# Retention block and mixture of experts on one core: slot biases summed on eight partitions, joined slot products, VectorE's order and two loads moved

## The chip, the cores and the metric

The kernel is written by hand for one core of a Trainium2 chip. Time is the device time of one execution in microseconds (us), and lower is better. Five engines work beside each other and meet only at semaphores: PE (TensorE, matrix products, whose weight loads have a row of their own, PEld), DVE (VectorE), ACT (ScalarE), POOL (GpSimd) and SP, which here issues the DMAs. Data lies in SBUF (128 partitions), products land in eight PSUM banks of 128 x 512 float32.

## The reference, cut to what matters

```python
x = L0_attn_x                                   # (4, 1024, 256)
x = x + attn(layernorm(x), ...)                 # retention with 16 heads of 16
x = x + ffn(layernorm(x), ...)

# attn: q, k, v = x @ W.T; scores decayed by head; y = (q k^T * decay / 4) v
mean, var = y.mean(axis=(1, 3)), y.var(axis=(1, 3))     # over time, per head
yn = (y - mean) / sqrt(var + EPS) * gn_weight + gn_bias
return yn @ W_o.T

# ffn: one shared expert, and 8 experts of which each token takes 2
shared = silu(xf @ sw1 + sb1) * (xf @ sw3 + sb3) @ sw2 + sb2
for k in range(2):
    exp_ids = (tok * 11 + k * 7919) % 8         # fixed by the token's number
    h = gelu(einsum('enc,ech->enh', xs, w1) + b1)
    y = einsum('enh,ehc->enc', h, w2) + b2
    out = out.at[sort_idx].add(y)
return (shared + out / 2) / 2
```

## The kernel before, in words

A token's two experts follow from its number modulo 8, so the host sorts each batch's 1024 tokens into eight *slots* of 128; slot s meets experts s and s-1. Every product is made in float32r with operands split in a high and a low part (`hi` and `lo`), as hi·hi + lo·hi + hi·lo: three matrix products where one stands in the reference (`split_product`, L305 in the profile's rows).

**First phase** (up to 213 us of the span): four batches in four parts of 256 tokens, so 16 parts, `step(0)` to `step(15)` on each engine. In step h, PE makes k and q of part h+1 (L305), state sums (L389), the two terms of y (L404, L413), transposes (L354 for k, L315 for x), v of part h+1, and the scores of part h+1 (L375). In the last two parts of a batch PE also multiplies the batch before by W_o (`output`). DVE in a step masks scores, adds and carries the state (`add_state`; `carry_state`, L827), scales k and q, makes the statistics of x of part h+3 (`ln_sums`), applies the layer norm (`ln_apply`, L781), and makes y's low part (`low_y`, L836), y's statistics (`y_sums`, L841) and x's low part for part h+2 (`low_x`, L786). `ln_apply` needs the reciprocal root that POOL makes from `ln_sums`; `low_y` needs ACT's high part of y; PE's next k needs `low_x`. From step 13 on, `ln2_sums` and `ln2_apply` (L948) do the same for the second layer norm, whose input `xl` is read back from a DRAM scratch.

POOL also makes low parts of the FFN's weights (L1087), adds the output bias to the residual, and in steps 0 and 1 forms the bias of each slot, `(sb2 + (b2[s] + b2[s-1]) / 2) / 2`, on all 128 partitions: b2 is loaded with each partition holding all eight rows, and `slot_bias_sums` (L1134) and `slot_bias_means` (L1138, L1140) work on 128 x 2048 numbers.

SP issues the loads in a written order: `load_x(h)` waits for the transposes of part h-4, and each is followed by a piece of the FFN's weights; `next_xres` loads 1 MB of residual, `store_x1` stores 1 MB.

**Second phase**: the shared expert and the experts. Per batch PE runs eight products `shared`, eight `expert`, and eight `slot`, the last of 8 chunks of contraction by 3 products of 256 columns, 24 in all, into the first half of `o_bank`; `add_slot` on DVE (L986) adds the bank to `xr`, which then is stored. Batches are three turns of a hardware loop and a last turn written out. Slot s waits until slot s-2's bank was read (`o_ready`).

Of the kernel before, what the change touches and what calls it, by code (L numbers as in the profile page):

```python
# [55 lines left out]

def moe_retention(nc, xa, xs, wattn, gnw, gnb, sw1, sw3, sw2, w1, w2, sb1, sb3, b1, sb2, b2, decay, masks, out):
    x1_dram = nc.dram_tensor("x1_scratch", [NBATCH, P, NE * D], F32).ap()
    last = NBATCH - 1

    with ExitStack() as ctx:
# [20 lines left out]
        sw2_split = SplitWeight(nc, ctx, "sw2", [P, MS, D], lo_first=True)  # L82
# [23 lines left out]
        w2_split = SplitWeight(nc, ctx, "w2", [P, NE, MR, D], lo_first=True)  # L106

        with ExitStack() as phase1:
# [17 lines left out]
            for i in range(2):  # L126
                yhi[i] = sb_1(f"yhi{i}", [P, GROUPS, NE, P], F32R)
                if i:

                    with nc.sbuf_tensor("slot_scratch", [P, 2, D], F32) as slot_scratch:  # L130
                        pass
                ylo[i] = sb_1(f"ylo{i}", [P, GROUPS, NE, P], F32R)
# [5 lines left out]
            sbias, bias7 = slot_scratch[:, 0, :], slot_scratch[:, 1, :]  # L138
# [21 lines left out]
        def expert_buffer(e):  # L160
# [28 lines left out]
        bias_ready, bias_part = sem("bias_ready"), sem("bias_part")  # L189
# [4 lines left out]
            sem(n) for n in ("h1_done", "h3_done", "sil_ready", "gf_ready", "ghi_ready", "glo_ready"))  # L194
        e_done, gelu_ready, ehi_ready, elo_ready, slot_done, biased, o_ready = (
# [15 lines left out]
        def _(sp):  # L211
# [53 lines left out]
            next_xres(0)  # L265
# [8 lines left out]
            load_ffn(10)  # L274
            sp.wait_ge(t_done, PARTS - 2)
# [23 lines left out]
        def _(pe):  # L299
            def split_product(o, w, x, first=True, last=True):  # L300

                n = len(w)
                for c in range(n):
                    for j, (l, r) in enumerate(((0, 0), (1, 0), (0, 1))):
                        mm = nc.tensor.matmul(o, w[c][l], x[c][r], start=first and c == 0 and j == 0,  # L305
                                              stop=last and c == n - 1 and j == 2)
                return mm
# [214 lines left out]
            def slot(b, s):  # L522
# [6 lines left out]
                w = [(sw2_split.hi[:, m, :], sw2_split.lo[:, m, :]) for m in range(MS)]  # L529
# [228 lines left out]
        def _(dve):  # L758
# [71 lines left out]
            def low_y(h):  # L830
                b, s = h // NSUP, h % NSUP
                at = slice(s * (SUPER // NE), (s + 1) * (SUPER // NE))
                if h == NSUP:
                    dve.wait_ge(bias_ready, 1)
# [4 lines left out]
            def y_sums(h):  # L839
                for g in range(GROUPS):  # L840
# [46 lines left out]
            def step(h):  # L887
# [25 lines left out]
                if b and s == 0:  # L913
                    gn_eps(b - 1, p_bank[0])
                if h + 3 < PARTS:
                    ln_apply(h + 3)
                elif h + 3 == PARTS:
                    ln2_apply(0, 0)
# [3 lines left out]
                low_y(h)  # L922
                y_sums(h)
                if h + 2 < PARTS:
                    low_x(h + 2)
                elif h + 2 == PARTS:
                    ln2_apply(0, 1)
# [54 lines left out]
            def add_slot(b, s):  # L982
# [3 lines left out]
                nc.vector.tensor_tensor(xr[:, s, :], o_bank[s % 2][:, 0:D], xr[:, s, :], ALU.add).then_inc(o_ready, 1)  # L986
# [70 lines left out]
        def _(pool):  # L1057
# [31 lines left out]
            def step(h):  # L1089
# [16 lines left out]
                if h == 0:  # L1106
                    slot_bias_sums()
                if h == 1:
                    slot_bias_means()
# [16 lines left out]
            def slot_bias_sums():  # L1126

                pool.wait_ge(bias_landed, 32)
                nc.gpsimd.tensor_scalar(sbias, sbias, 0.5, None, ALU.mult)
                nc.gpsimd.tensor_copy(bias7, slot_bias[:, NE - 1, :]).then_inc(bias_part, 1)  # L1130
                for i, s in enumerate(reversed(range(NE))):
                    pool.wait_ge(bias_part, i + 1)
                    before = slot_bias[:, s - 1, :] if s else bias7
                    nc.gpsimd.tensor_tensor(slot_bias[:, s, :], slot_bias[:, s, :], before, ALU.add).then_inc(bias_part, 1)  # L1134

            def slot_bias_means():
                pool.wait_ge(bias_part, NE + 1)
                nc.gpsimd.tensor_scalar(slot_bias[:], slot_bias[:], 0.25, None, ALU.mult).then_inc(bias_part, 1)  # L1138
                pool.wait_ge(bias_part, NE + 2)
                nc.gpsimd.tensor_tensor(slot_bias[:], slot_bias[:], sbias.unsqueeze(1).broadcast_to([P, NE, D]), ALU.add).then_inc(bias_ready, 1)  # L1140
# [11 lines left out]
            pool.wait_ge(bias_ready, 1)  # L1152
# [69 lines left out]
```

## Time and profile before

| | |
|---|---|
| median of 3 runs | 455.54 us (454.89 to 456.48) |
| the profiled execution's own time | 458.03 us |
| its span | 456.2 us |
| PE busy | 442.1 us, 97% of the span |
| DVE, ACT, POOL busy | 286.2, 216.7, 109.3 us |
| granted TensorE clock, mean | 0.989 |

The span is the stretch from the first to the last instruction in the trace; the execution's own time holds 1.8 us around it. The profiled execution took 2.5 us more than the median of the three runs without a profile. Times in rows are us from the span's start.

### The profile page before, as it was taken

How to read it: one execution, taken by the hardware profiler on the slowest of the kernel's cores; microseconds unless marked ns; L12 is line 12 of the kernel's file. 1: busy time of each engine (PE TensorE's matmuls, PEld its weight loads, DVE VectorE, ACT ScalarE, POOL GpSimd, SP SyncE). 2: the span in 40 equal slices, each digit the busy share in tenths (PEclk: the TensorE clock that was granted, in tenths of full speed). 3: DMA queues.
4: the chain of work that ended last, by engine and by line, in shares of the span. 5: the costliest groups of instructions: out<-in, count | busy, mean ns of one | idle time of the engine just before them, and what ended most of it. 6: DMA issues, size and time to landing. Idle time of an engine off the chain costs nothing.

```text
span 456.2 us, 14962 instructions
## 1 busy us (share of the span) xinstructions
PE 442.1 (97%) x6574; PEld 408.3 (90%) x6574; DVE 286.2 (63%) x653; ACT 216.7 (47%) x416; POOL 109.3 (24%) x81
## 2 busy tenths in 40 slices
PE   6999798999999999999999999999999999999997
PEld 4999798999899998898889999899998899988997
DVE  6888786767777777867565633856347473465321
ACT  3556356544664657544428233463334643336521
POOL 1168322522134223414180200402004010040000
PEclk9999898999999999899999999999999999999999
DMA  8512242201632042100622011400115001120011
GB/s 261 210 51 74 70 158 79 71 24 53 208 121 72 5 134 103 49 3 37 242 102 83 1 47 56 177 0 0 46 46 184 0 0 46 43 95 0 1 47 46
DMA packets 9990, 34.75 MB, mean 76 GB/s; under 512 B 1744, under 2 KB 2128, under 8 KB 8272
## 3 DMA queue, kind: packets, MB, share of 16 engines
q1 hardware_dynamic: 9504, 33.15, 20.6%
q8 instruction: 45, 0.74, 0.7%
q10 hardware_dynamic: 432, 0.79, 0.6%
q14 instruction: 9, 0.07, 0.0%
HBM read 25.54 MB, written 8.39 MB: 74 GB/s over the span
## 4 chain that ended last, share of the span: by engine, by line
PE 90%; DVE 4%; issue 3%; POOL 1%; DMA 1%; ACT 1%; POOLq 0%; DVEq 0%; ACTq 0%
PE bank L305 70%; PE bank L375 5%; PE bank L404 3%; PE bank L413 3%; PE bank L389 3%; PE bank L354 2%; PE bank L492 2%; PE bank L315 1%; DMA xin<-xa 1%; DVE state L827 1%; PE bank L429 1%; DVE xlo L786 1%; POOL w_lo L1087 1%; DVE y_st L841 0%; DVE ylo L836 0%
## 5 line engine op out<-in xcount | busy, mean ns | idle before, releaser
L708 ACT ACTIVATE xres<-bank,r1b 128x256 f32<-128x256 f32 x64 | 26.7, 468 | 55.6 <-PE bank L305 55.6
L305 PE MATMUL bank<-x2hi,sw_lo 128*128 128x512 f32 x128 | 51.0, 398 | 0.0
L305 PE MATMUL bank<-x2hi,sw_hi 128*128 128x512 f32 x128 | 50.8, 397 | 0.0
L693 ACT ACTIVATE sil<-bank,s1b 128x512 f32<-128x512 f32 x32 | 22.0, 688 | 60.4 <-PE bank L305 60.4
L305 PE MATMUL bank<-x2lo,sw_hi 128*128 128x512 f32 x128 | 50.2, 392 | 0.0
L968 DVE SCALAR_TENSOR_TENSOR gf<-bank,s3b,sil 128x512 f32<-128x512 f32 x32 | 23.9, 746 | 34.6 <-PE bank L305 34.6
L305 PE MATMUL bank<-xhi,wqkv_hi 128*128 128x256 f32 x128 | 40.2, 314 | 3.9 <-DVE xlo L786 3.7
L802 DVE TENSOR_TENSOR pm<-bank,msk 128x512 f32<-128x512 f32 x64 | 39.8, 683 | 5.9 <-PE bank L375 5.8
L625 ACT ACTIVATE keo<-kT,msk 128x512 f32<-128x512 f32 x32 | 21.3, 714 | 46.0 <-DVE kT L791 46.0
L986 DVE TENSOR_TENSOR xr<-bank,xr 128x256 f32<-128x256 f32 x32 | 13.5, 423 | 41.9 <-PE bank L305 41.9
L1121 POOL TENSOR_TENSOR xr<-xr,slot_bias 128x2048 f32<-128x2048 f32 x4 | 18.5, 4625 | 82.2 <-DMA xr<-x_scratch 82.2
L974 DVE TENSOR_TENSOR glo<-gf,ghi 128x512 fp32r<-128x512 f32 x32 | 34.8, 1087 | 3.7 <-ACT ghi L697 3.7
L305 PE MATMUL bank<-xhi,wqkv_lo 128*128 128x256 f32 x128 | 37.0, 289 | 0.0
L305 PE MATMUL bank<-xlo,wqkv_hi 128*128 128x256 f32 x128 | 36.9, 289 | 0.0
L305 PE MATMUL bank<-x2lo,w_hi 128*128 128x256 f32 x128 | 36.2, 283 | 0.0
L305 PE MATMUL bank<-x2hi,w_hi 128*128 128x256 f32 x128 | 36.2, 283 | 0.0
L305 PE MATMUL bank<-x2hi,w_lo 128*128 128x256 f32 x128 | 36.2, 283 | 0.0
L980 DVE TENSOR_TENSOR elo<-xres,ehi 128x512 fp32r<-128x512 f32 x32 | 22.1, 691 | 22.5 <-ACT ehi L712 22.5
L305 PE MATMUL bank<-sw_hi,ghi 128*128 128x256 f32 x128 | 36.2, 282 | 0.0
L305 PE MATMUL bank<-w_hi,elo 128*128 128x256 f32 x128 | 36.1, 282 | 0.0
L305 PE MATMUL bank<-w_lo,ehi 128*128 128x256 f32 x128 | 36.0, 281 | 0.0
L305 PE MATMUL bank<-w_hi,ehi 128*128 128x256 f32 x128 | 35.9, 281 | 0.0
(120 smaller groups left out, 1265.9 us busy)
## 6 DMA issues: line engine op xcount, KB each, us to landing
xin<-xa SPq DMA_DIRECT2D x16, 256.0 KB, 3.2
w_raw<-w SPq DMA_DIRECT2D x8, 512.0 KB, 4.2
xres<-xs SPq DMA_DIRECT2D x4, 1024.0 KB, 5.0
x_scratch<-xres SPq DMA_DIRECT2D x4, 1024.0 KB, 5.5
xl<-x_scratch SPq DMA_DIRECT2D x8, 512.0 KB, 5.5
xr<-x_scratch SPq DMA_DIRECT2D x4, 1024.0 KB, 4.9
out<-xr SPq DMA_DIRECT2D x7, 512.0 KB, 2.6
sw_raw<-sw SPq DMA_DIRECT2D x3, 512.0 KB, 5.0
```

Source lines behind the costliest of these rows:

```text
L305: mm = nc.tensor.matmul(o, w[c][l], x[c][r], start=first and c == 0 and j == 0, stop=last and c == n - 1 and j == 2)
L375: mm = nc.tensor.matmul(p_bank[p][:, o:o + CH], keo[at, c, g, :, :], qT[h % 2][at, g, c * CH:(c + 1) * CH], start=True, stop=True)
L389: mm = nc.tensor.matmul(a_bank[32 * p:32 * p + 32, o:o + n * 32].rearrange("p (n e) -> p n e", n=n), kexp[:, c, r, :], vexp[h % 2][:, c, r ...
L404: nc.tensor.matmul(y_bank[at, o:o + CH], state[h % 2][at, g, c, :], qT[h % 2][at, g, c * CH:(c + 1) * CH], start=(c == first and g == 0), ...
L625: cp = nc.scalar.activation(keo[:, :, :, odd, :], kT[:].rearrange("p g (c j) -> p c g j", c=CPS), ACT.Copy, scale=parity[:, odd:odd + 1])
L693: nc.scalar.activation(sil[i % 2][:], h1_bank[i % 2][:], ACT.Silu, bias=s1b[:, m:m + 1]).then_inc(sil_ready, 1)
L708: ge = nc.scalar.activation(hf[q % 2][:, m, :], e_bank[q % 4][:, m * 2 * P:(m + 1) * 2 * P], ACT.Gelu, bias=r1b[:, e, m:m + 1])
L802: nc.vector.tensor_tensor(pm[p][:], p_bank[p][:].rearrange("p (a i) -> p a i", i=CH), causal.unsqueeze(1).broadcast_to([P, CPS * GROUPS, C ...
L968: nc.vector.scalar_tensor_tensor(gf[i % 3][:], h3_bank[i % 2][:], s3b[:, m:m + 1], sil[i % 2][:], ALU.add, ALU.mult).then_inc(gf_ready, 1)
L974: nc.vector.tensor_tensor(glo[half][:, m, :], gf[i % 3][:], ghi[half][:, m, :].bitcast(F32), ALU.subtract).then_inc(glo_ready, 1)
L980: nc.vector.tensor_tensor(elo[k][:], hf[q % 2][:], ehi[k][:].bitcast(F32), ALU.subtract).then_inc(elo_ready, 1)
L1121: nc.gpsimd.tensor_tensor(xr[:], xr[:], slot_bias[:], ALU.add).then_inc(biased, 1)
```

## The change

Five edits.

1. **Slot biases.** b2, b2 shifted by one row and sb2 are loaded onto eight partitions (one for each slot), POOL does four operations of 8 x 256 in step 1, the result is stored to a DRAM scratch, and later broadcast to 128 partitions by a DMA of 1 MB, behind the last piece of weights and ahead of the first `xl` load.
2. **The residual's first load** (`next_xres(0)`, 1 MB) moves forward, from behind `load_ffn(4)` to behind the small bias loads of part 2's group.
3. **DVE's order in a step**: `low_y` and `y_sums` go ahead of `ln_apply` (or `ln2_apply`) and of the residual. In step 15 `y_sums` and `gn_channels` go ahead of the residual, and `low_y` behind it.
4. **Joined slot products**: high and low part of w2 and sw2 lie in one tensor, and one product of 512 columns takes both against the high part of the activations. A slot has 16 products.
5. **`add_slot`** adds the two halves of the bank, one after the other, with a semaphore between them.

```diff
+class JoinedWeight:
+    def __init__(self, nc, ctx, name, shape):
+        p, n, *rest = shape
+        with ExitStack() as at:
+            at.enter_context(nc.sbuf_tensor(name + "_before", shape, F32))
+            self.raw = at.enter_context(nc.sbuf_tensor(name + "_raw", shape, F32))
+        self.both = ctx.enter_context(nc.sbuf_tensor(name + "_both", [p, 2 * n, *rest], F32R))
+        self.hi, self.lo = self.both[:, 0:n], self.both[:, n:2 * n]
...
-            sp.dma_start(slot_bias[:], b2.partition_broadcast(P)).then_inc(bias_landed, 16)
-            sp.dma_start(sbias, sb2.partition_broadcast(P)).then_inc(bias_landed, 16)
+            sp.dma_start(bias_in[:, 0, :], b2).then_inc(bias_landed, 16)
+            sp.dma_start(bias_in[1:NE, 1, :], b2[0:NE - 1]).then_inc(bias_landed, 16)
+            sp.dma_start(bias_in[0:1, 1, :], b2[NE - 1:NE]).then_inc(bias_landed, 16)
+            sp.dma_start(bias_in[:, 2, :], sb2.partition_broadcast(NE)).then_inc(bias_landed, 16)
             load_x(6)
             sp.dma_start(wo_raw[:], wattn[:, 3]).then_inc(w_landed[3], 16)
             for dst, src in ((s1b, sb1), (s3b, sb3), (r1b, b1)):
                 sp.dma_start(dst[:], src).then_inc(c2_landed, 16)
+            next_xres(0)
             load_x(7)
...
             load_ffn(3)
+            sp.wait_ge(bias_part, 4)
+            sp.dma_start(bias_dram, bias_in[:, 0, :]).then_inc(bias_stored, 16)
             load_x(9)
             load_ffn(4)
-            next_xres(0)
...
             load_ffn(10)
+            sp.wait_ge(bias_stored, 16)
+            sp.dma_start(slot_bias[:], bias_dram.partition_broadcast(P)).then_inc(slots_landed, 16)
             sp.wait_ge(t_done, PARTS - 2)
             load_xl(0, 0)
...
+            def wide_product(o, x, w):
+                n = len(w)
+                for c in range(n):
+                    hi, lo = x[c]
+                    nc.tensor.matmul(o.rearrange("p (k d) -> p k d", k=2), hi, w[c], start=c == 0, stop=c == n - 1, skip_group_check=True)
+                    mm = nc.tensor.matmul(o[:, 0:D], lo, w[c][:, 0, :], start=False, stop=c == n - 1, skip_group_check=True)
+                return mm
...
-                    w += [(w2_split.hi[:, e, m, :], w2_split.lo[:, e, m, :]) for m in range(MR)]
-                split_product(o_bank[s % 2][:, 0:D], g, w).then_inc(slot_done, 1)
+                    w += [w2_split.both[:, e::NE, m, :] for m in range(MR)]
+                wide_product(o_bank[s % 2][:], g, w).then_inc(slot_done, 1)
...
                 dve.wait_ge(slot_done, b * NE + (s + 1))
-                nc.vector.tensor_tensor(xr[:, s, :], o_bank[s % 2][:, 0:D], xr[:, s, :], ALU.add).then_inc(o_ready, 1)
+                nc.vector.tensor_tensor(xr[:, s, :], o_bank[s % 2][:, 0:D], xr[:, s, :], ALU.add).then_inc(o_half, 1)
+                dve.wait_ge(o_half, b * NE + (s + 1))
+                nc.vector.tensor_tensor(xr[:, s, :], o_bank[s % 2][:, D:2 * D], xr[:, s, :], ALU.add).then_inc(o_ready, 1)
...
+            def slot_biases():
+                pool.wait_ge(bias_landed, 64)
+                at = bias_in[:, 0, :]
+                nc.gpsimd.tensor_tensor(at, at, bias_in[:, 1, :], ALU.add).then_inc(bias_part, 1)
...
+                nc.gpsimd.tensor_scalar(at, at, 0.5, None, ALU.mult).then_inc(bias_part, 1)
```

The order on DVE is taken from the compiled programs. In step 13, the second part of the last batch, DVE issued before (`xl` is the second layer norm's input, `ylo` y's low part, `y_st` its statistics, `xlo` the low part that PE's next k and v products need, `pm` the masked scores of the next step):

```order
L936 BN_STATS ln_st<-xl 128x6 x4
L940 BN_AGGR ln_mv<-ln_st 128x2 x4
L943 TENSOR_SCALAR ln_ve<-ln_mv 128x4
L948 TENSOR_SCALAR xl<-xl,ln_mv,ln_r 128x256 x4
L836 TENSOR_TENSOR ylo<-bank,yhi 128x16x32
L841 BN_STATS y_st<-bank 128x6 x2
L786 TENSOR_TENSOR xlo<-bank,xhi 128x512
```

and now:

```order
L972 BN_STATS ln_st<-xl 128x6 x4
L976 BN_AGGR ln_mv<-ln_st 128x2 x4
L979 TENSOR_SCALAR ln_ve<-ln_mv 128x4
L866 TENSOR_TENSOR ylo<-bank,yhi 128x16x32
L872 BN_STATS y_st<-bank 128x6 x2
L984 TENSOR_SCALAR xl<-xl,ln_mv,ln_r 128x256 x4
L816 TENSOR_TENSOR xlo<-bank,xhi 128x512
```

The application of the layer norm, which waits for POOL's `ln_r`, now stands behind the two operations on y; `xlo` stays last.

On SP, around the constants of part 2's group, the order was (`wo_raw` is W_o, `s1b`, `s3b` and `r1b` small biases):

```order
L256 DMA wo_raw<-wattn 128x512
L258 DMA s1b<-sb 128x4
L258 DMA s3b<-sb 128x4
L258 DMA r1b<-b 128x16
L215 DMA xin<-xa 128x512
```

and it is now:

```order
L273 DMA wo_raw<-wattn 128x512
L275 DMA s1b<-sb 128x4
L275 DMA s3b<-sb 128x4
L275 DMA r1b<-b 128x16
L243 DMA xres<-xs 128x2048
L229 DMA xin<-xa 128x512
```

The 1 MB load of the residual follows the constants with no wait between them. At the end of the loads of the first phase SP now has, where the third of these rows was not there before:

```order
L229 DMA xin<-xa 128x512
L234 DMA w_raw<-w 128x1024
L295 DMA slot_bias<-bias_scratch 128x2048
L253 DMA xl<-x_scratch 128x1024
L238 DMA x_scratch<-xres 128x2048
```

So 1 MB of broadcast now follows 0.75 MB of x and weights at once, and the load of `xl` keeps its own wait behind it.

## Rows read from the trace of the kernel before

**Rows 1.** The page's chain of work that ended last, by engine.
```profile
PE 90%; DVE 4%; issue 3%; POOL 1%; DMA 1%; ACT 1%; POOLq 0%; DVEq 0%; ACTq 0%
```

**Rows 2.** The chain in order of time, 38 to 56 us: start, us, what.
```profile
40.29 0.83 PE bank L389 x64
41.12 1.64 PE bank L305 x12
...
51.59 2.89 PE bank L305 x12
54.47 1.12 PE bank L389 x64
```

**Rows 3.** The timeline, 42 to 52 us: start, us, engine, line, operation; idle time before it.
```profile
42.06 4.59 POOL L1140 TENSOR_TENSOR slot_bias<-slot_bias,slot_scratch 128x2048 f32<-128x2048 f32 x1
43.39 3.44 DVE L827 TENSOR_SCALAR state<-state,msk 128x32 f32<-128x32 f32 x2
51.59 0.54 PE L305 MATMUL bank<-xhi,wqkv_hi 128*128 128x256 f32 x1 [2.38 <-DVE xlo L786]
```

**Rows 4.** Busy times by stretch: us, PE, PEld, DVE, ACT, POOL, PEclk, DMA share, GB/s.
```profile
51.60:55.50 3.90, 3.90 (x76) 3.66 (x76) 2.33 (x4) 0.00 (x0) 0.63 (x1) 0.56 0.02 6
```

**Rows 5.** POOL's timeline in step 0.
```profile
27.08 5.61 POOL L1134 TENSOR_TENSOR slot_bias<-slot_bias 128x256 f32<-128x256 f32 x7
```

**Rows 6.** The chain, 59 to 75 us.
```profile
59.86 1.44 PE bank L305 x12
...
69.79 1.43 issue
...
72.43 2.57 PE bank L305 x12
```

**Rows 7.** SP's timeline: the issues of three loads.
```profile
28.40 0.43 SPq L258 DMA_DIRECT2D r1b<-b  x1
...
62.61 0.43 SPq L229 DMA_DIRECT2D xres<-xs  x1
...
138.30 0.43 SPq L220 DMA_DIRECT2D w_raw<-w  x1
```

**Rows 8.** DMA queues, 61.9 to 68.6 us, then 68.6 to 69.7: packets, MB, share.
```profile
q1 hardware_dynamic: 423, 1.80, 76.2%
...
q8 instruction: 1, 0.02, 5.4%
```

**Rows 9.** DVE and PE in step 13, from the timeline.
```profile
187.78 1.38 DVE L948 TENSOR_SCALAR xl<-xl,ln_mv,ln_r 128x256 f32<-128x256 f32 x4 [1.12 <-POOL ln_r L1117]
...
191.08 0.38 PE L305 MATMUL bank<-xhi,wqkv_hi 128*128 128x256 f32 x1 [0.76 <-DVE xlo L786]
```

**Rows 10.** The chain, 188 to 195 us.
```profile
189.16 0.60 DVE ylo L836
189.76 0.67 DVE y_st L841 x2
...
191.08 2.52 PE bank L305 x12
193.59 1.44 PE bank L389 x64
```

**Rows 11.** PE behind step 15, from the timeline.
```profile
216.96 0.38 PE L419 MATMUL bank<-y_mv,msk 128*128 128x2 f32 x2 [0.55 <-DVE y_mv L847]
```

**Rows 12.** PE's timeline: first and last of 46 products of 256 columns, then of 22 of 512.
```profile
227.03 0.28 PE L305 MATMUL bank<-wo_lo,yhi 128*128 128x256 f32 x1
...
232.42 0.28 PE L305 MATMUL bank<-wo_lo,yhi 128*128 128x256 f32 x1
220.79 0.40 PE L305 MATMUL bank<-x2lo,sw_hi 128*128 128x512 f32 x1
...
225.70 0.39 PE L305 MATMUL bank<-x2lo,sw_hi 128*128 128x512 f32 x1
```

**Rows 13.** The end of the chain.
```profile
453.17 0.42 DVE xr L986
```

More of the change, by code:

```diff
@@ L81, in moe_retention @@
         sw3_split = SplitWeight(nc, ctx, "sw3", [P, CB, HS])
-        sw2_split = SplitWeight(nc, ctx, "sw2", [P, MS, D], lo_first=True)
+        sw2_split = JoinedWeight(nc, ctx, "sw2", [P, MS, D])
         msk = sb("msk", [P, MASK_W])
@@ L105, in moe_retention @@
         w1_split = SplitWeight(nc, ctx, "w1", [P, NE, CB, HR], lo_first=True)
-        w2_split = SplitWeight(nc, ctx, "w2", [P, NE, MR, D], lo_first=True)
+        w2_split = JoinedWeight(nc, ctx, "w2", [P, NE, MR, D])
         with ExitStack() as phase1:
@@ L128, in moe_retention @@
                 if i:
-                    with nc.sbuf_tensor("slot_scratch", [P, 2, D], F32) as slot_scratch:
+                    with nc.sbuf_tensor("slot_scratch", [P, 3, D], F32) as slot_scratch:
                         pass
@@ L137, in moe_retention @@
             o_bias = sb_1("o_bias", [P, D])
-            sbias, bias7 = slot_scratch[:, 0, :], slot_scratch[:, 1, :]
+            bias_in = slot_scratch[0:NE]
         xl = sb("xl", [P, NE, D])
@@ L188, in moe_retention @@
         xl_landed = [sem(f"xl{i}_landed") for i in range(2)]
-        bias_ready, bias_part = sem("bias_ready"), sem("bias_part")
+        bias_part, bias_stored, slots_landed = sem("bias_part"), sem("bias_stored"), sem("slots_landed")
         ln2_stats, ln2_aggr, ln2_var, ln2_rstd, xn2_ready = (
@@ L194, in moe_retention @@
             sem(n) for n in ("h1_done", "h3_done", "sil_ready", "gf_ready", "ghi_ready", "glo_ready"))
+        o_half = sem("o_half")
         e_done, gelu_ready, ehi_ready, elo_ready, slot_done, biased, o_ready = (
@@ L528, in slot @@
                 g = [(ghi[half][:, m, at], glo[half][:, m, at]) for m in range(MS)]
-                w = [(sw2_split.hi[:, m, :], sw2_split.lo[:, m, :]) for m in range(MS)]
+                w = [sw2_split.both[:, m::MS, :] for m in range(MS)]
                 if s == 0:
@@ L833, in low_y @@
                 if h == NSUP:
-                    dve.wait_ge(bias_ready, 1)
+                    dve.wait_ge(bias_stored, 16)
                 dve.wait_ge(yhi_ready, h + 1)
@@ L839, in y_sums @@
             def y_sums(h):
+                dve.wait_ge(yhi_ready, h + 1)
                 for g in range(GROUPS):
@@ L914, in step @@
                     gn_eps(b - 1, p_bank[0])
+                if h + 1 == PARTS:
+                    y_sums(h)
+                    gn_channels(b)
+                    for j in (2, 3):
+                        residual(b - 1, j, p_bank[j])
+                    low_y(h)
+                    return
+                low_y(h)
+                y_sums(h)
                 if h + 3 < PARTS:
                     ln_apply(h + 3)
-                elif h + 3 == PARTS:
-                    ln2_apply(0, 0)
+                else:
+                    ln2_apply(0, h + 3 - PARTS)
                 if b and s >= 2:
@@ L1105, in step @@
                     pool.wait_ge(xn2_ready, h + 4 - PARTS)
-                if h == 0:
-                    slot_bias_sums()
                 if h == 1:
-                    slot_bias_means()
+                    slot_biases()
                 if b and s == 1:
@@ L1124, in experts @@
                     ln2_power(b + 1, 1)
[L1126 to L1140, printed above, removed]
+            def slot_biases():
+                pool.wait_ge(bias_landed, 64)
+                at = bias_in[:, 0, :]
+                nc.gpsimd.tensor_tensor(at, at, bias_in[:, 1, :], ALU.add).then_inc(bias_part, 1)
+                pool.wait_ge(bias_part, 1)
+                nc.gpsimd.tensor_scalar(at, at, 0.5, None, ALU.mult).then_inc(bias_part, 1)
+                pool.wait_ge(bias_part, 2)
+                nc.gpsimd.tensor_tensor(at, at, bias_in[:, 2, :], ALU.add).then_inc(bias_part, 1)
+                pool.wait_ge(bias_part, 3)
+                nc.gpsimd.tensor_scalar(at, at, 0.5, None, ALU.mult).then_inc(bias_part, 1)
             nc.gpsimd.memset(minus_half[:], -0.5).then_inc(half_set, 1)
@@ L1151, in _ @@
             bias_xres(last)
-            pool.wait_ge(bias_ready, 1)
+            pool.wait_ge(slots_landed, 16)
             with pool.Fori(0, last) as b:
```

5 lines of the change are left out of this document (1 added, 4 removed).

## Prediction

> **What bounds the kernel now.** I read the page's chain first: PE holds 90% of it, DVE 4%, POOL and DMA 1% each, and 3% is "issue" [rows 1]. So PE's own work sets nearly all of the time. An edit pays only where it shortens that work or closes one of the few gaps in it. I then went through the chain in order of time and marked each piece that is not PE's, and each PE piece that takes longer than its twins. Four places remain.
>
> *The gap in step 2.* POOL's last operation on the slot biases takes 4.59 us from 42.06. DVE's `carry_state`, two instructions on 32 numbers each, starts at 43.39 and takes 3.44 us, ending when POOL ends [rows 3]. Everything behind it on DVE is late, `xlo` last, and PE waits 2.38 us at 51.59 [rows 3]. The engine then runs for 3.9 us at a granted clock of 0.56 [rows 4], which is mostly the lower level of 1.2 GHz. Twelve products take 2.89 us where 1.64 is usual, the state sums 1.12 where 0.83 is usual [rows 2]: 1.5 us more. The place costs 2.4 + 1.5 = 3.9 us.
>
> *The gap in step 4.* PE stops for 1.43 us with no engine to release it, in the middle of a run of like products with no wait between them. The twelve products after it take 2.57 us, against 1.44 for the same twelve a step earlier [rows 6], so the clock fell again; with the transposes behind them I count 1.5 us, as in step 2. I looked for what the queues did. 1.80 MB moved between 61.9 and 68.6 us, at 76% of all 16 engines, and no packet of the instruction queue; directly behind it, in 68.6 to 69.7, comes one of 16 KB [rows 8]. The last load of that burst is `next_xres(0)`, issued at 62.61 [rows 7]. My reading is that PE's next piece of code stood behind the burst. The place costs 2.9 us.
>
> *The gap in step 13.* DVE idles 1.12 us for POOL's `ln_r`, then applies the layer norm in 1.38 us [rows 9], then makes `ylo` (0.60) and `y_st` (0.67) [rows 10], then `xlo`; PE waits 0.76 us for that [rows 9]. The lower clock follows: 2.52 against 1.64 and 1.44 against 0.83 [rows 2, 10], 1.5 us. The place costs 2.3 us.
>
> *The gap behind step 15*: 0.55 us for the last statistics of y [rows 11].
>
> **The change part by part.**
>
> *Slot biases on eight partitions.* In step 0 the seven additions of 256 columns took 5.61 us, 0.8 each [rows 5]. Four operations of that width should take 3.2 us. Fewer partitions need not make them shorter (lower bound some 0.4 each, if they do). They begin where the first of the two wide operations began, so that the four are over before the second one's old start at 42.06. The `carry_state` that was held starts at 43.39 [rows 3], and is free. The gap in step 2 goes: **-3.9 us** (bounds -2.4, if another gap still draws the lower clock, and -3.9). What follows in its place is `xlo` as in other steps, with no wait in them. SP waits for POOL's fourth operation before `load_x(9)`. Queued behind are all later loads; but SP comes to that wait behind `load_x(8)`, which needs a transpose of PE's step 2, a whole step after POOL's four operations, so it costs 0. If POOL were late, x of part 9 would be late next, which is used four steps on.
>
> The Trainium skill says the same of the pair of engines (SBUF — State Buffer, section "SBUF: two separate sides"): GpSimd and a VectorE operation in a two-port mode hold a shared port for a whole instruction, and the other blocks. By that rule also the four small operations could hold DVE, but for one of them at a time; the 3.44 us agree.
>
> *The order on DVE.* In step 13 `ylo` and `y_st` (1.27 us together) now fill the 1.12 us of waiting for `ln_r`. `xlo` is therefore ready some 1.1 us sooner, which covers PE's 0.76. The gap and its slow stretch go: **-2.3 us**. Bounds: 0, if DVE comes late from something else, and -2.3. The margin is only 0.3. In step 15 the statistics pass the residual: **-0.6** (0 to -0.6). In the other steps PE has no wait on DVE that ended a gap, so the order changes nothing there; what hides it is PE's scores, which stand between the transposes and the products that need `xlo`. Against it: in step 14 the residual's two additions stand behind the 1.38 us application and y's operations, and the next scores need their banks: **+0.1** (0 to 0.5).
>
> *Joined products.* Products of 256 columns follow each other at (232.42 - 227.03) / 45 = 0.1198 us, those of 512 at (225.70 - 220.79) / 21 = 0.2338 [rows 12]. A chunk took 3 x 0.1198 = 0.3594 and takes 0.2338 + 0.1198 = 0.3536. That is 0.0058 less, and 32 slots of 8 chunks are 256: **-1.5 us** (bounds 0 and -2.0 by the scatter of such rows). The columns are the same. No row shows a product that reads its moving operand in two stretches 16 KB apart; see the rival.
>
> *`add_slot` in two halves.* One addition is 0.42 us [rows 13]. In the loop DVE idles for PE before each, so a second one hides behind the next slot's 8 x 0.354 = 2.8 us of products, and banks alternate. If that cover were gone it would cost 32 x 0.45 = 14 us. At the end nothing hides it: 0.42 and a semaphore, **+0.45 us**.
>
> *The loads.* The xres load leaves the burst at 62 us, which keeps 0.75 MB: the gap in step 4 goes, **-2.9** (0 to -2.9). But it is now issued right behind `r1b`, at about 28.9 [rows 7], behind 0.5 MB and the constants. And the broadcast of 1 MB is issued right behind a w_raw load at 138.30 [rows 7], behind 0.75 MB. That is the burst of 62 us over again, to the kilobyte, at about the same point of a step. I give it what that one cost, **+2.9** (0 to 4.4; a wait of 2.9 in place of 1.43, and the slow stretch). For the earlier, smaller one I take **+2.0**, between nothing and the same 2.9, nearer to it because PE executes code fastest in just those steps. The burst that held the broadcast of b2 before loses 1.1 MB, and the chain has no gap there: 0.
>
> The Trainium skill speaks against these three terms (Runtime: NRT & Kernel Launch, "Instruction fetch mechanics"): a block of 16 KiB holds 256 instructions, and crossing to the next is "mostly hidden". The size agrees with the row of the instruction queue; the hiding does not fit the 1.43 us. By the rule the loads would change nothing.
>
> **The sum**, against the profiled execution of 458.03 us (span 456.2 and 1.8 around it): -3.9 - 2.3 - 0.6 + 0.1 - 1.5 + 0.45 = -7.75 for the engines; -2.9 + 2.9 + 2.0 = +2.0 for the loads. Together -5.7, and 452.3 in a profile. The median of the unprofiled runs is 2.5 lower, 455.54, and gives **449.8 us**.
>
> **The rivals.**
> - *Late code at neither place, or only at the first.* The requests may fall before the new load's descriptors are queued. Then -7.75 - 2.9 and 0 to 2.0: 444.9 to 446.9. For it: the constants take SP 0.43 us each, and the broadcast follows its neighbour by as much, so a request can slip between. Against it: the same burst was caught at 62 us.
> - *Both places in full*, each 4.4 us with its slow stretch: -7.75 - 2.9 + 8.8 = -1.9, 453.7. For it: the waits would be as long as the burst, 6.7 us [rows 8], less one piece of code.
> - *Code is never late* (the page's rule, as a mechanism of this kernel): the 1.43 us have a cause that stays, and the loads are free. -7.75 gives 447.8.
> - *The joined product is slow* (the other side). If reading in two stretches, or writing both halves, cost a product more than 5.7 / 256 = 22 ns, the change would be slower than before; at 0.1 us each it is +26, 476 us. Against it: the products of 512 columns in rows 12 fill a whole bank, and run at 0.457 ns a column.
> - *`carry_state` is held again*, by POOL's residual bias in step 13, which starts behind the application of the layer norm and so later beside PE's earlier step: some 1 us, within the range.
>
> **How the numbers follow.** Forecast (late code once or twice in part, 448 to 452): 0.42. Rival one: 0.25. Rival two, 452 to 454.5: 0.16. Rival three: 0.09. Slow joined products or another loss: 0.08. The range of 444.8 to 453.8 leaves out the last and the edge of rival two. Within 0.3% of before (about what a measurement of this kernel can tell from no change) is 454.2 to 456.9: 0.06 from rival two and the losses; slower 0.06; faster 0.88.
>
> **What would show it.** Step 2's `carry_state` at 0.4 us and no PE idle at 51 us; no gap in step 13; `xlo` there ahead of PE; a pair in a slot at 0.354 us; two DVE additions at the end. For the loads: PE idle "issue" near 34 to 36 us and about 141 to 144 us (all earlier by the gaps closed), each with an instruction packet at the end of a burst, and none in step 4. If step 4 keeps its gap with the burst gone, my reading of it is wrong. If the joined products run at over 0.26 us, the sum is.

## The result

The changed kernel takes **449.34 us** (median of 4 runs, 448.79 to 449.88) beside 455.22 us for the kernel before (4 runs, 454.71 to 456.48) on the same chip: ratio 0.9867, interval 0.9842 to 0.9891. It was timed twice more, on other chips: 449.08 us, ratio 0.9869 (0.9835 to 0.9904), and 448.55 us, ratio 0.9859 (0.9817 to 0.9901). So it is faster by 6 to 7 us. The prediction was 449.8 us in a range of 444.8 to 453.8. Medians and ranges below hold every run; a ratio leaves out one execution, of 453.4 us under all_bursts_short, in which the chip was in a slower state.

The profiled execution took 449.29 us (span 447.5), 8.7 us less than the profiled one of before; the medians are 5.9 apart. That difference matters below.

From the page of the changed kernel, busy times and the chain by engine, which answers to [rows 1]:

```profile
PE 437.0 (98%) x6318; PEld 392.8 (88%) x6318; DVE 296.8 (66%) x685; ACT 216.6 (48%) x416; POOL 95.5 (21%) x73
...
PE 96%; DMA 1%; issue 1%; DVE 1%; ACT 0%; POOL 0%; DVEq 0%; ACTq 0%
```

PE holds 96% of the chain, 90% before. DVE and POOL have nearly left it; the gaps in which PE waited for another engine are gone. By stretch (us, busy time and count of each engine, granted clock, DMA share, GB/s):

```profile
8.00:12.00 4.00, 3.85 (x16) 3.27 (x17) 3.31 (x8) 1.11 (x2) 0.00 (x0) 0.57 0.98 294
33.00:36.00 3.00, 1.90 (x110) 1.57 (x109) 2.06 (x8) 1.18 (x2) 0.43 (x1) 1.00 0.21 82
43.00:52.00 9.00, 9.00 (x265) 8.41 (x254) 6.85 (x19) 5.80 (x13) 2.77 (x2) 1.00 0.18 49
183.00:190.00 7.00, 7.00 (x193) 6.46 (x195) 6.06 (x14) 2.98 (x8) 5.01 (x4) 1.00 0.24 77
```

Steps 2 and 13 (third and fourth row) have PE busy throughout at the full clock; [rows 3, 4, 9, 10] showed a gap and a stretch at the lower one in both. The second row shows 1.1 us that PE does not fill. The first row holds the only stretch at the lower clock in this execution, in the prologue; the profile of before had the full clock there.

The timeline of POOL, DVE and PE at the places that changed:

```profile
39.28 0.72 POOL L1166 TENSOR_TENSOR slot_scratch<-slot_scratch 8x256 f32<-8x256 f32 x1 [3.02 <-DVE xin L811]
...
41.84 0.84 POOL L1172 TENSOR_SCALAR slot_scratch<-slot_scratch 8x256 f32<-8x256 f32 x1
...
45.64 0.38 DVE L857 TENSOR_SCALAR state<-state,msk 128x32 f32<-128x32 f32 x2
...
50.18 0.69 DVE L816 TENSOR_TENSOR xlo<-bank,xhi 128x512 fp32r<-128x512 f32 x1 [0.43 <-ACT xhi L632]
...
181.68 0.17 DVE L979 TENSOR_SCALAR ln_ve<-ln_mv 128x4 f32<-128x4 f32 x1
181.80 0.69 DVE L866 TENSOR_TENSOR ylo<-bank,yhi 128x512 fp32r<-128x512 f32 x1
182.41 0.75 DVE L872 BATCH_NORM_STATS2 y_st<-bank 128x6 f32<-128x256 f32 x2
183.07 1.36 DVE L984 TENSOR_SCALAR xl<-xl,ln_mv,ln_r 128x256 f32<-128x256 f32 x4
...
266.30 0.39 PE L335 MATMUL bank<-sw_both,ghi 128*128 128x512 f32 x1
...
269.81 0.40 PE L335 MATMUL bank<-sw_both,ghi 128*128 128x512 f32 x1
```

POOL's four operations of 8 x 256 run from 39.28 to 42.68 us and end ahead of `carry_state`, which takes 0.38 us where it took 3.44. In step 13 the two operations on y fill the wait for `ln_r`, and the application follows them with no idle time. The last two rows are ten chunks apart, across the end of a slot: 3.51 / 10 = 0.351 us for a pair of products, one of 512 columns and one of 256.

The chain in order of time: the start, the two new stops of PE that no engine releases, the place behind step 15 where [rows 11] had 0.55 us, and the end:

```profile
9.07 1.71 PE bank L589 x4
10.78 4.82 PE bank L326 x36
...
34.17 0.70 PE bank L443 x40
34.87 1.10 issue
35.97 0.54 PE bank L443 x24
...
139.18 0.69 issue
139.87 0.64 PE bank L434 x29
...
206.38 3.00 PE bank L326 x12
209.38 0.12 PE bank L449 x2
209.50 2.91 PE bank L326 x12
...
444.30 0.43 DVE xr L1022
...
444.76 0.42 DVE xr L1024
```

The stop in step 4 ([rows 6], 1.43 us and a stretch at the lower clock) is gone, and 1.10 and 0.69 us stand behind the two loads that the prediction named (the second at 139.18 us, a little ahead of the 141 to 144 given), with no stretch at the lower clock behind either. Two more stops of this kind were there before and still are: 1.01 us at 123.26 is now 0.47 at 118.39, and 0.69 at 171.55 is now 0.39 at 167.04. Together the stops came to 3.1 us before and come to 2.7 us now. The instruction queue in 33.4 to 33.8 us and in 137.5 to 138.0 us (packets, MB, share):

```profile
q8 instruction: 1, 0.02, 14.5%
q8 instruction: 1, 0.02, 11.2%
```

The load queue was busy ahead of each: it moved 0.84 MB in 30 to 33 us at a share of 93%, and 0.77 MB in 136 to 138 us at 101%. The first packet starts at 33.79 us, and next to nothing of its burst is left behind it; the second starts at 137.52, and another 0.27 MB follow it in 138.0 to 138.8 us, so it comes near the end of its burst and not behind it. PE resumes at 35.97 and 139.87, 2.2 and 2.4 us behind the packet's start. In the kernel before, the packet started at 68.75 us and PE resumed at 71.22, 2.5 us later.

### The profile page after: what moved, and what is told of

It reads as the page before. It is cut to its first block, busy times and chain, and to the rows that moved or that the text cites. A ratio compares the mean times of both kernels' runs of the same rounds, so it can differ in the third digit from the quotient of the medians.

```text
span 447.5 us, 14478 instructions
## 1 busy us (share of the span) xinstructions
PE 437.0 (98%) x6318; PEld 392.8 (88%) x6318; DVE 296.8 (66%) x685; ACT 216.6 (48%) x416; POOL 95.5 (21%) x73
## 4 chain that ended last, share of the span: by engine, by line
PE 96%; DMA 1%; issue 1%; DVE 1%; ACT 0%; POOL 0%; DVEq 0%; ACTq 0%
PE bank L326 52%; PE bank L335 13%; PE bank L336 7%; PE bank L405 7%; PE bank L443 4%; PE bank L434 4%; PE bank L419 3%; PE bank L384 2%; PE bank L345 2%; PE bank L522 2%; DMA xin<-xa 1%; PE bank L459 1%; PE bank L589 0%; ACT kexp L640 0%; PE bank L449 0%
## 5 line engine op out<-in xcount | busy, mean ns | idle before, releaser
L335 PE MATMUL bank<-sw_both,ghi 128*128 128x512 f32 x128 | 46.5, 396 | 0.0
L335 PE MATMUL bank<-w_both,ehi 128*128 128x512 f32 x128 | 46.4, 397 | 0.0
L1010 DVE TENSOR_TENSOR glo<-gf,ghi 128x512 fp32r<-128x512 f32 x32 | 36.2, 1130 | 2.6 <-ACT ghi L727 2.6
L336 PE MATMUL bank<-sw_both,glo 128*128 128x256 f32 x128 | 35.9, 281 | 0.0
L336 PE MATMUL bank<-w_both,elo 128*128 128x256 f32 x128 | 35.9, 281 | 0.0
```

The costliest lines, as they stand in the source:

```text
L335: nc.tensor.matmul(o.rearrange("p (k d) -> p k d", k=2), hi, w[c], start=c == 0, stop=c == n - 1, skip_group_check=True)
L336: mm = nc.tensor.matmul(o[:, 0:D], lo, w[c][:, 0, :], start=False, stop=c == n - 1, skip_group_check=True)
L1010: nc.vector.tensor_tensor(glo[half][:, m, :], gf[i % 3][:], ghi[half][:, m, :].bitcast(F32), ALU.subtract).then_inc(glo_ready, 1)
```

## The experiments

Differences of 1 us are near what such runs can tell. So a place's own rows in the profile are read beside each median. The chips differ a little too: the kernel before had a median of 454.17 us on the chip of order_back, xres_back, split_products and biases_back, 455.26 on that of short_bursts, changed_again, extra_burst and eight_short_operations, 454.89 on that of all_bursts_short and order_alone, and 455.23 on that of changed_third and order_back_again.

**order_back**: the changed kernel with the order on VectorE of before.

```diff
-                low_y(h)
-                y_sums(h)
...
-                else:
-                    ln2_apply(0, h + 3 - PARTS)
+                elif h + 3 == PARTS:
+                    ln2_apply(0, 0)
...
+                low_y(h)
+                y_sums(h)
```

> The changed kernel with VectorE's order of before; all other edits kept. Theory: the gap of step 13 comes back, VectorE idling about 1.1 us for GpSimd's root ahead of the application and PE waiting some 0.3 to 0.8 us for x's low part, perhaps with a stretch at the lower clock behind it, and 0.5 us behind step 15. Median 1.0 to 2.9 us above the changed kernel (450.3 to 452.2). Rival: with the gap of step 2 gone the last steps have slack, the order is worth nothing, and the time is within 0.3 us of the changed kernel.

450.55 us (448.66 to 454.03, 10 runs), ratio 0.9924 (0.9892 to 0.9957), inside the range expected, but on another chip than the changed kernel. Its timeline on DVE and PE:

```profile
183.62 1.38 DVE L979 TENSOR_SCALAR xl<-xl,ln_mv,ln_r 128x256 f32<-128x256 f32 x4 [1.12 <-POOL ln_r L1148]
...
186.18 0.67 DVE L816 TENSOR_TENSOR xlo<-bank,xhi 128x512 fp32r<-128x512 f32 x1
...
186.91 0.39 PE L326 MATMUL bank<-xhi,wqkv_hi 128*128 128x256 f32 x1 [0.76 <-DVE xlo L816]
```

The 1.12 and 0.76 us are [rows 9] over again. But behind the 0.76 the clock did not fall: the mean granted clock of this execution is 1.000. The same gap drew a stretch at the lower clock in the profile of before [rows 10].

**changed_third** and **order_back_again**: the same two versions beside each other on one chip.

> The changed kernel once more, on the same chip as the version with the order on VectorE put back, since the two were timed on different chips so far. Theory (the order is worth its two gaps, 0.76 and 0.55 us, and in part of the executions a stretch at the lower clock of some 1.5 us): a median 1.2 to 2.3 us below that version's. Rival (the difference of 1.2 us between medians of two chips was the chips'): less than 0.5 us apart. For the whole change both expect a ratio of 0.985 to 0.990 to the kernel before.

> The changed kernel with the order on VectorE of before, repeated beside the changed kernel. Theory: 450.3 to 451.6 us, with PE waiting 0.76 us for xlo in step 13 and 0.55 us for the statistics of y behind step 15. Rival: within 0.5 us of the changed kernel in this call, though the two waits are there, because PE's stops behind bursts of loads take up the slack.

448.55 us (448.18 to 450.24) and 450.38 us (449.25 to 452.99), 6 runs each; ratios 0.9859 (0.9817 to 0.9901) and 0.9896 (0.9851 to 0.9942). The order is worth 1.8 us, and the rival of a difference under 0.5 us falls. The two waits of PE, 0.76 and 0.54 us in the profile of the second, are 1.3 of it.

**order_alone**: the kernel before with the new order on VectorE and nothing else (its diff is that of order_back with the signs turned, and one wait for `yhi` more in `y_sums`).

> The kernel before with VectorE's new order alone. Theory: the gap of step 13 (0.76 us) and the one behind step 15 (0.55) go, that of step 2 stays at 1.5 to 2.4 us and that of step 4 at 1.3 to 1.7. 1.3 us below before, or 2 to 3 where the lower clock had followed step 13. Rival: the order also shortens the chain of step 2, since y's two operations (1.27) fill the wait for GpSimd's root (0.84) there, and takes 0.8 us off its gap; 2.1 us below before.

453.13 us (451.15 to 454.62, 10 runs) against 454.89, ratio 0.9951 (0.992 to 0.9982): again 1.8 us. Step 2 on DVE and PE:

```profile
44.43 3.88 DVE L827 TENSOR_SCALAR state<-state,msk 128x32 f32<-128x32 f32 x2
...
52.13 0.58 PE L305 MATMUL bank<-xhi,wqkv_hi 128*128 128x256 f32 x1 [1.88 <-DVE xlo L786]
```

The waits in step 13 and behind step 15 are gone. In step 2 `carry_state` is still held, and PE's wait is 1.88 us instead of 2.38, since there too the operations on y now fill a wait. That half microsecond is of the kind that the rival of this run named (it had 0.8) and my sum had not; it is a gain only as long as the slot biases stay wide. Behind the wait the lower clock came again: the twelve products took 2.93 us.

**biases_back**: the changed kernel with the slot biases formed on 128 partitions again, as before.

```diff
-            sp.dma_start(slot_bias[:], bias_dram.partition_broadcast(P)).then_inc(slots_landed, 16)
...
+                if h == 0:
+                    slot_bias_sums()
                 if h == 1:
-                    slot_biases()
+                    slot_bias_means()
```

> The changed kernel with the slot biases formed on 128 partitions by GpSimd, as before, and without the late broadcast; all other edits kept. Theory: the state's carry in step 1 is held until GpSimd's last wide operation ends, PE idles 1 to 2.4 us at about 50 us, and the lower clock follows; the stop at 139 us (0.69) goes. 1.5 to 3.5 us above the changed kernel, 450.8 to 452.8. Rival: the new order on VectorE alone has hidden the gap of step 2 (y's operations ahead of the application save 0.8 us in the same chain); then PE idles under 0.5 us there, and the kernel is as fast as the changed one or faster by 0.7.

451.25 us (450.11 to 454.8, 10 runs), ratio 0.9944 (0.9908 to 0.9981). On POOL, DVE and PE:

```profile
43.99 4.59 POOL L1170 TENSOR_TENSOR slot_bias<-slot_bias,slot_scratch 128x2048 f32<-128x2048 f32 x1
...
44.87 3.89 DVE L849 TENSOR_SCALAR state<-state,msk 128x32 f32<-128x32 f32 x2
...
52.57 0.39 PE L318 MATMUL bank<-xhi,wqkv_hi 128*128 128x256 f32 x1 [1.88 <-DVE xlo L808]
```

The hold is back (3.89 us until POOL ends), and with it PE's wait and a stretch at the lower clock (the twelve products behind it take 2.46 us); the stop at 139 us is not there. It is 0.7 us slower than order_back on the same chip, which was 1.8 slower than the changed kernel: 2.5 us for this part. From the ratios to before, 0.9944 against 0.9867, it is 3.5. Either figure is net of what the broadcast costs at 139 us, which this version does without.

**eight_short_operations**: the kernel before, its last wide operation on POOL cut into eight.

```diff
-                nc.gpsimd.tensor_tensor(slot_bias[:], slot_bias[:], sbias.unsqueeze(1).broadcast_to([P, NE, D]), ALU.add).then_inc(bias_ready, 1)
+                for s in range(NE):
+                    tt = nc.gpsimd.tensor_tensor(slot_bias[:, s, :], slot_bias[:, s, :], sbias, ALU.add)
+                tt.then_inc(bias_ready, 1)
```

> The kernel before with GpSimd's last wide operation on the slot biases (128 x 2048, 4.6 us) written as eight of 128 x 256 in a row; the sum is the same. Theory (VectorE is held for one whole GpSimd instruction): the state's carry in step 1 takes at most 1.3 us in place of 3.4, though GpSimd is busy as long or longer (5.6 us), and PE's wait at 51 us falls under 0.5 us. Rival (GpSimd's work slows VectorE as long as it lasts): the carry ends when GpSimd does, 4 us or more, and PE waits 3 us.

453.4 us, one run, so only its rows are read. POOL, DVE and PE:

```profile
41.95 5.56 POOL L1141 TENSOR_TENSOR slot_bias<-slot_bias,slot_scratch 128x256 f32<-128x256 f32 x8
...
43.47 1.32 DVE L827 TENSOR_SCALAR state<-state,msk 128x32 f32<-128x32 f32 x2
...
47.47 0.71 POOL L1065 TENSOR_TENSOR ln_r<-ln_ve,minus_half 128x2 f32<-128x2 f32 x1
...
48.23 0.73 DVE L781 TENSOR_SCALAR xin<-xin,ln_mv,ln_r 128x256 f32<-128x256 f32 x2 [2.06 <-POOL ln_r L1065]
...
50.87 0.58 PE L305 MATMUL bank<-xhi,wqkv_hi 128*128 128x256 f32 x1 [1.59 <-DVE xlo L786]
```

Half of the expectation held. `carry_state` is held for 1.32 us, about as long as its two instructions and parts of two short operations of 0.7 us, and no longer for a whole wide one. But PE still waits 1.59 us, where I expected under 0.5, and the lower clock follows (2.93 us for the twelve products). The missing reason is in the third and fourth rows: POOL takes its queue in order, the eight operations occupy it until 47.5 us, and `ln_r`, whose input `ln_ve` was ready at 46.16 us, comes behind them. So the wide operations cost in two ways, by the hold and by the queue; making them short cures one, having them done by 42.68 us cures both.

**xres_back**: the changed kernel with the residual's first load at its old place.

```diff
                 sp.dma_start(dst[:], src).then_inc(c2_landed, 16)
-            next_xres(0)
...
             load_ffn(4)
+            next_xres(0)
```

> The changed kernel with the residual's first load at its old place, behind the load of weights of step 3. Theory (PE's code waits behind a long burst of loads): the stop of 1.1 us at 34.9 us goes, and PE stops again in step 4, by 1.0 to 1.5 us at about 65 to 70 us, with an instruction packet at the burst's end. Median within 1 us of the changed kernel, or 1.5 above if the lower clock follows. Rival (the stops belong to places of the program): the stop at 34.9 stays where it is and none comes in step 4.

449.03 us (447.52 to 451.41, 4 runs), ratio 0.989 (0.9826 to 0.9953), within 1 us of the changed kernel as expected. Its chain:

```profile
65.13 0.70 PE bank L443 x40
65.82 1.70 issue
67.53 0.54 PE bank L443 x24
...
68.65 1.44 PE bank L326 x12
```

The stop left 34.9 us and is back in step 4, with 1.70 us (1.0 to 1.5 expected). All eight profiles of kernels with the residual's load at its new place have a stop at 33.7 to 34.9 us, of 1.10 to 1.65 us; none of the other six has one there. The twelve products behind it take 1.44 us, at the full clock; behind 1.43 us of the same stop they took 2.57 in the profile of before [rows 6].

**extra_burst**: the changed kernel with another megabyte loaded behind `load_ffn(4)`, into a buffer that is overwritten later.

```diff
+            sp.dma_start(slot_bias[:], b2.partition_broadcast(P)).then_inc(extra_landed, 16)
```

> The changed kernel with one load more: b2 broadcast to the 128 partitions, 1 MB, behind the weights of step 3, where the residual's load stood before; nothing waits for it but SP before the late broadcast. Theory: the burst of 1.75 MB is there again and PE stops in step 4, at 65 to 69 us, by 1.0 to 1.7 us; the other stops are unchanged. Rival: the stop in step 4 was due to the residual's load itself (its place in memory, or someone waiting for it) and does not come.

452.24 us, one run, read by its rows. Its chain:

```profile
66.82 0.69 PE bank L445 x40
67.51 2.15 issue
69.66 0.54 PE bank L445 x24
...
70.79 2.34 PE bank L328 x12
```

A different load at the same place gives the same stop, at the same product (the 41st of 64), so it is the burst and not the residual's data. It is longer than the 1.7 us expected at most, and the lower clock follows it (2.34 us for twelve products). Its packet started at 67.26 us.

**split_products**: the changed kernel with 24 products of 256 columns in a slot and one addition.

```diff
-                    w += [w2_split.both[:, e::NE, m, :] for m in range(MR)]
-                wide_product(o_bank[s % 2][:], g, w).then_inc(slot_done, 1)
+                    w += [(w2_split.hi[:, e, m, :], w2_split.lo[:, e, m, :]) for m in range(MR)]
+                split_product(o_bank[s % 2][:, 0:D], g, w).then_inc(slot_done, 1)
```

> The changed kernel with 24 products of 256 columns in a slot and one addition, as before; all other edits kept. Theory: a slot takes 2.87 us in place of 2.82, and the end is 0.45 us shorter; 0.6 to 1.1 us above the changed kernel, 449.9 to 450.4. Rival: joining is worth more, since it also spares 256 weight loads; then 2 us or more above.

449.75 us (448.49 to 450.77, 4 runs), ratio 0.99 (0.9851 to 0.9949). Its timeline on PE:

```profile
267.19 0.28 PE L326 MATMUL bank<-sw_both,glo 128*128 128x256 f32 x1
...
268.97 0.29 PE L326 MATMUL bank<-w_both,elo 128*128 128x256 f32 x1
```

These two are five chunks apart, 0.356 us each, against 0.351 joined. Rows so few apart overstate it a little: the mean over the 233 distances between neighbouring chunks that nothing interrupts is 0.3506 us joined and 0.3539 us split (0.3539 also in the kernel before), so 0.0033 us a chunk. The medians are 0.4 to 1.2 us above the changed kernel's three, in the direction expected and inside the scatter.

**changed_again**: the changed kernel once more.

> The changed kernel itself once more, as a yardstick on the same chip. Both theories: 449.3, give or take 1, with stops of PE at 35, 118, 139 and 167 us that add up to 2 to 4 us.

449.08 us (447.3 to 450.51, 6 runs), ratio 0.9869 (0.9835 to 0.9904). Its chain has stops again, but not all of the same ones: 1.10 us at 33.73, 1.29 at 117.26, 0.41 at 124.71, 0.39 at 166.44, and none near 139, where I had expected one. They come to 3.2 us; in the profile of changed_third they come to 2.8.

**short_bursts**: the two moved loads cut in halves, each issued in the middle of a step, when PE's q is done.

```diff
+            def half_xres(i, turn):
+                sp.wait_ge(q_done, turn)
...
-            next_xres(0)
+            half_xres(0, 4)
+            half_xres(1, 5)
...
-            sp.dma_start(slot_bias[:], bias_dram.partition_broadcast(P)).then_inc(slots_landed, 16)
+            half_slots(0, 13)
+            half_slots(1, 14)
```

> The changed kernel with the residual's first load and the slots' broadcast each cut into two halves of 0.5 MB, and each half issued in the middle of a step (behind PE's q product), apart from the 0.75 MB of x and weights. Theory: PE's stops at 34.9 us and at 139 us go and none comes in their place, since no burst is longer than PE's code in hand; those at 118 and 167 us, behind the stores of x1, stay. 1.3 to 2.5 us below the changed kernel, about 447.5. Rival: what counts is the megabytes near a piece of code, not the length of one burst; then the stops come at other places and the time is within 0.5 us of the changed kernel.

448.72 us (446.59 to 449.86, 6 runs), ratio 0.9869 (0.9837 to 0.99). Both stops are gone in its profile, and so is the one at 167 us; only one is left, which stands behind the store of x1:

```profile
116.19 1.29 issue
117.48 1.60 PE bank L338 x12
```

That execution was its fastest, 446.59 us. The median is 0.4 us below the changed kernel's on the same chip, and the ratios are equal; I had expected 1.3 to 2.5, and the rival's "within 0.5 us" is what the times show. Of the two stops only the first can be called this edit's doing, since changed_again had none at 139 us either.

**all_bursts_short**: the same, with the first store of x1 in halves too.

```diff
-            store_x1(0)
+            half_store(0, 9)
...
+            half_store(1, 10)
```

> short_bursts with the first store of x1 cut into halves too, the first issued in the middle of step 7, the second in the middle of step 8. Theory: PE's last stop of over 1 us, at 116 us, goes as well; the load of the residual's next batch (1 MB alone, behind the second half) costs at most 0.5 us. 0.5 to 1.5 us below short_bursts, some 447.6. Rival: that stop is not the burst's (it would stay at 116 us), and the time is short_bursts' 448.7 within 0.3.

449.42 us (446.64 to 453.4, 6 runs), ratio 0.9844 (0.9796 to 0.9892). The stop at 116 us is gone, but the profiled execution, of 453.2 us, has a new one:

```profile
57.91 1.95 issue
...
62.05 3.62 PE bank L426 x64
65.67 2.86 PE bank L347 x12
```

It stands behind half a residual, 0.5 MB, with the packet of code at the burst's end (it started in 57.0 to 57.5 us). After it the lower clock holds for some 10 us (64 products in 3.62 us where 1.94 is usual). The single runs were 446.64, 447.32, 448.38, 450.46, 453.2 and 453.4. So halves do not rid the kernel of stops for good: a block of code can meet a short burst too. Without the run of 453.4 us, which the ratio leaves out, the median is 448.38 us. By the ratios, 0.9844 here and 0.9869 for short_bursts, each inside the other's interval, whether this version is any better is not settled; the 0.5 to 1.5 us expected are not shown.

## Why the prediction was right, step by step

The time was right to half a microsecond, and that closeness is luck. The gaps and their causes were named rightly; their sizes were not: the engines' terms were summed too high and the loads' too high the other way.

- **The gap in step 2, -3.9.** The mechanism was right: free `carry_state`, no wait, no lower clock (windows and timeline above). The runs give 2.5 to 3.5 us, which fits two things that the term left out: once DVE's order is changed the gap is 1.88 us and not 2.38, and the broadcast at times costs a stop of its own. The 1.5 us for the stretch at the lower clock were fair at this place: it stands behind this gap in all four profiles that have it (2.38, 1.88, 1.88 and 1.59 us, in before, biases_back, order_alone and eight_short_operations), though three of biases_back's ten runs had a mean clock of 0.999 and so hardly had it.
- **The stretch at the lower clock elsewhere.** The sum charged it in full at each place, from one execution. Behind the gap of step 13 it stands in one profile of four (0.76 or 0.77 us in before, order_back, order_back_again and eight_short_operations). Of the 47 stops of PE of 0.3 us or more that no engine ended, counted over all 14 profiles from 15 us on, three have it behind them (1.43, 1.95 and 2.15 us). The profiled execution of before had three such stretches [rows 4, 6, 10] and a mean clock of 0.989; of its 58 runs in these comparisons only four had 0.989 (mean 457.2 us), 25 had 0.995 or 0.996 (454.3), 24 had 0.991 to 0.993 (455.8), five had 0.999 or more (452.1). Of the changed kernel's 16 runs, 13 had 0.999 or more (448.8) and three 0.996 (450.0). So a mean clock lower by 0.003 to 0.004 goes with 1.2 to 2.2 us, and the changed kernel, with fewer gaps, has fewer such stretches; but a gap does not bring one each time.
- **The price of the small operations.** I took 3.2 us for four; they took 3.40, so eight partitions made them no shorter, as 0.8 each for 128 partitions [rows 5] said. That they would be over before "the second one's old start at 42.06" missed by 0.6 us: POOL starts them behind DVE's layer norm, which the new order puts later (39.28 us here, 36.88 in order_back). It did not matter: `carry_state` came at 45.64.
- **The order on DVE, -2.3, -0.6 and +0.1.** Mechanism right at both places: 0.76 and 0.55 us gone, and back in order_back. Together -2.8 in the sum, and 1.8 us in two comparisons: the waits are 1.3 of it in both, and of the rest the shorter wait in step 2 explains 0.5 in order_alone alone; in the other it is inside the scatter. The rest of the difference is the stretch at the lower clock, charged in full. The 0.1 for the residual in step 14 is too small for these runs.
- **Joined products, -1.5, and the addition, +0.45.** By the means over the whole phase a pair takes 0.3506 us and a split chunk 0.3539, so 0.85 us over 256; the term took 0.3594 for the split one, from products of `output`, which was too slow by 0.0055. The end has two additions, 0.43 and 0.42 (chain above). Net that is 0.4 us, where the sum had 1.05. The medians, 0.4 to 1.2 us apart, agree and don't prove it by themselves. The moving operand in two stretches 16 KB apart costs nothing that shows: the rival of slow joined products is dead.
- **The loads, -2.9, +2.9 and +2.0.** The reading of `issue` as late code held in both runs that moved or added a burst, and all 47 stops fit it (last section). The forecast's own case, "late code once or twice in part", is what the profiles of the changed kernel have. Both places were named rightly. But the sizes were too large: 1.10, 1.10 and 1.38 us in three profiles of the changed kernel at 34 us, and 0.69, none and none at 139 us, all without the lower clock. Over the eight profiles that have this broadcast in one piece, three have the stop at 139 us: 0.69, 0.38 in xres_back and 1.17 in split_products. What was removed was smaller too: step 4 cost 1.43, 0.96 and 1.27 us in three profiles of kernels with the old loads, with a slow stretch in the first alone. Taken together, the stops come to 3.1 us in the profile of before and to 2.7, 3.2 and 2.8 us in three of the changed kernel. Moving the residual's load is about zero (xres_back is 0.3 us below to 0.5 us above the changed kernel's medians, with its stop elsewhere), where the sum had +2.0. The step that failed is "I give it what that one cost": the price of one caught request in one execution was put on the other places in full.

So -7.75 for the engines should have been about -4.7 to -5.7 (2.5 to 3.5, 1.8, 0.4), and +2.0 for the loads about 0. The errors cancelled. That leaves 0.2 to 2.0 of the 5.9 to 6.7 us measured, which no run assigns; the slow stretch behind step 4, which the changed kernel's profiles lack, is a candidate, and so is the scatter. The rival "code is never late" would have given 447.8 and is refuted by xres_back and extra_burst, though its time was only 1.5 us off; a median alone could not have told these apart. The Trainium skill calls the crossing from one block to the next "mostly hidden" (Runtime: NRT & Kernel Launch, "Instruction fetch mechanics"). The page of the changed kernel counts 44 packets in the larger instruction queue, and at most five stops of PE of 0.3 us or more of this kind stand in any of these traces, the longest of 2.15 us: mostly hidden is so, and the rest is what these loads move about.

Open: what decides whether a gap of PE draws the lower clock (0.76 us did in one execution and did not in another; 1.43 did and 1.70 did not), and what decides how far into a burst the packet comes. At 139 us the cases lie less than a microsecond apart: in changed_again and changed_third the packet started at 136.64 and 136.70 us, also inside the burst, and PE did not stop; in the first profile it started at 137.52. Also not tried: joined weights that lie contiguously, high part beside low part, which would tell whether the two stretches cost a nanosecond.

## What to carry to other kernels

Price a gap of PE at its own length first, and a stretch at the lower clock behind it at its chance, not in full (here four of four at one place, one of four at another, three of 47 behind stops for code); look at the mean clock of several runs before taking one profile's stretches for the rule. When small work on GpSimd runs beside short VectorE work, ask both how long one instruction holds the other engine and what stands behind it in GpSimd's queue; shrinking it to the partitions that are distinct answers both. When PE stops with no releaser in the middle of like products, look for an instruction packet late in a burst of loads before suspecting a semaphore: such a stop moves with the load, so moving a load gained nothing by itself here.

## What the runs showed of the hardware

- At all 47 stops of PE that no engine ended (0.32 to 2.15 us), PE resumed 2.2 to 2.5 us behind the start of the last packet of the larger instruction queue. At the 12 waits that DVE ended the same distance ran from 1.8 to 4.9 us. So a stop's length fits how late its packet came; that was read from traces, not tried by itself.
- A burst of 0.53 MB was enough for the longest stop but one, 1.95 us, and one of 1.8 MB gave only 0.69: the size of the burst did not predict the stop.
- Operations of POOL on 256 columns took 0.72 to 0.85 us on eight partitions, and 0.70 us (5.56 / 8) to 0.80 [rows 5] on 128.
